# Second layer's attention: query projections moved to the second and third step of a batch

## The reference, cut to what matters

```python
x = x + _attention(_rmsnorm(x, g1), wq, wk, wv, wo)      # this stage
# in _attention, per batch:
q = (x @ wq).reshape(B, S, 16, 16).transpose(0, 2, 1, 3) # query projections
k = (x @ wk)...; v = (x @ wv)...                         # 4 heads each
q = q * cos + _rotate_half(q) * sin                      # rotary turn
k = k * cos + _rotate_half(k) * sin
scores = einsum('bhqd,bhkd->bhqk', q, k) / sqrt(16), causal
out = softmax(scores) @ v ... @ wo
```

## Time and profile before

| | |
|---|---|
| three timed runs | 3857.84, 3857.79, 3856.64 us; median 3857.79 |
| profiled execution | 3857.93 us, its span 3856.1 us |
| TensorE busy, share of the span | 3439.5 us, 89% |
| VectorE, ScalarE, GpSimd busy | 2474.5, 2175.3, 1169.2 us |
| mean granted TensorE clock | 0.938 of full speed |

### The profile page before, as it was taken

How to read it: one execution, slowest core, us unless ns; L and a number is a source line. 1 busy time by engine, 2 the same in 40 slices (tenths; PEclk the granted TensorE clock), 3 DMA queues, 4 the chain that set the end, 5 groups by cost and what they waited for, 6 DMA issues and landing times. The chain is left out here.

```text
span 3856.1 us, 68147 instructions
## 1 busy us (share of the span) xinstructions
PE 3439.5 (89%) x19130; PEld 2597.4 (67%) x19130; DVE 2474.5 (64%) x7055; ACT 2175.3 (56%) x5066; POOL 1169.2 (30%) x1802
## 2 busy tenths in 40 slices
PE   2999999999999999989999968867878775799996
PEld 2777777777777777768888834445555555688885
DVE  5777777777777777766666633345555545566665
ACT  1777777777777777746555521124545441355553
POOL 1333333333333333333343300032122200343442
PEclk9999999999999999999999967878989895899998
DMA  4222222222222222243343311110001014355454
GB/s 156 44 48 48 48 48 48 48 48 48 46 45 46 48 48 48 48 162 122 120 142 120 120 39 33 33 40 20 24 22 25 21 28 151 120 137 137 118 140 150
DMA packets 177636, 282.42 MB, mean 73 GB/s; under 512 B 32498, under 2 KB 119282, under 8 KB 177522
## 3 DMA queue, kind: packets, MB, share of 16 engines
q1 hardware_dynamic: 162930, 261.03, 23.4%
q0 software_dynamic: 14592, 19.93, 3.1%
HBM read 161.89 MB, written 41.16 MB: 53 GB/s over the span
## 5 line engine op out<-in xcount | busy, mean ns | idle before, releaser
L723 POOL TENSOR_SCALAR at_p<-at_p,at_recip 128x128 f32<-128x128 f32 (+3 forms) x1028 | 533.6, 532 | 983.3 <-DVE at_recip L862 983.3
L773 ACT ACTIVATE at_p<-at_p,at_nmax 128x128 f32<-128x128 f32 (+3 forms) x1030 | 575.8, 559 | 290.4 <-DVE at_nmax L856 287.3
L856 DVE CUSTOM_DVE_ANT_0 at_p<-at_s_ps,at_bias 128x128 f32<-128x128 f32 (+3 forms) x1030 | 493.7, 479 | 154.1 <-PE at_s_ps L971 154.1
L978 PE MATMUL at_t_ps<-ident,at_p 128*128 128x128 f32 x2560 | 459.7, 278 | 0.4 <-POOL at_p L723 0.4
L1745 DVE CUSTOM_DVE_ANT_0 aa_a_ps<-aa_a_ps,aa_hidden 128x128 f32<-128x128 f32 (+3 forms) x512 | 247.2, 507 | 273.7 <-PE aa_a_ps L1909 269.7
L970 PE MATMUL at_s_ps<-at_k_twice,at_q 128*128 128x128 f32 (+3 forms) x1030 | 387.8, 377 | 8.1 <-DVE at_nmax L856 1.2
L1645 ACT ACTIVATE aa_pT<-aa_b_ps 128x512 f32<-128x512 f32 (+1 forms) x384 | 196.2, 528 | 281.8 <-PE aa_b_ps L1927 277.8
L971 PE MATMUL at_s_ps<-at_k_twice,at_q 128*128 128x128 f32 (+3 forms) x1030 | 332.3, 323 | 0.0
L978 PEld LDWEIGHTS at_t_ps<-ident,at_p 128*128 128x128 f32 x2560 | 294.9, 140 | 46.2 <-DVE at_pT L869 30.0
L988 PE MATMUL at_o_ps<-at_pT,at_v 128*64 128x512 f32 (+3 forms) x2064 | 306.3, 439 | 0.0
L970 PEld LDWEIGHTS at_s_ps<-at_k_twice,at_q 128*128 128x128 f32 x1030 | 194.4, 189 | 91.0 <-DVE at_nmax L856 44.5
(11 more groups left out here) (316 smaller groups left out, 8639.1 us busy)
## 6 DMA issues: line engine op xcount, KB each, us to landing
at_k_twice<-at_k_parts SPq DMA_DIRECT2D x260, 256.0 KB, 3.3
nw_w_raw<-in_w_all_dram SPq DMA_DIRECT2D x52, 1024.0 KB, 7.5
w_raw<-in_w_dram SPq DMA_DIRECT2D x57, 768.0 KB
ln_x<-in_x_dram SPq DMA_DIRECT2D x10, 512.0 KB, 4.8
nw_xh<-xh_dram SPq DMA_DIRECT2D x10, 512.0 KB, 4.3
nw_xl<-xl_dram SPq DMA_DIRECT2D x10, 512.0 KB, 4.9
rc_x<-x_dram SPq DMA_DIRECT2D x10, 512.0 KB, 3.8
at_w_raw<-in_w_heads_dram SPq DMA_DIRECT2D x18, 256.0 KB, 3.4
```

What stands on the lines that cost most here:

```text
L723: pool.tensor_scalar(p, p, recip[:, u:u + 1], 1.0, ALU.mult, ALU.mult).then_inc(scaled, 1)
L773: act.activation(p_sb[:, u, 0:N], p_sb[:, u, 0:N], ACT.Exp, bias=nmax[:, u:u + 1], scale=-1.0, accum_out=total[:, u:u + 1]).then_inc(exped, 1)
L856: dve.tensor_tensor_reduce(out=p_sb[:, u, 0:N], in0=s_ps[u % 2][:, 0:N], in1=bias[:, u % 2, S - N:S], scale=1.0, scalar=BIG, op0=ALU.add, ...
L978: ins = pe.transpose(t_ps[u % 2][:, k * P:k * P + P], p_sb[:, u, k * P:k * P + P], ident[:])
```

## The change

The table NEXT is rewritten. q0 goes from (2,0) to (1,1), q1 from (10,0) to (2,1), kk from (1,1) to (2,0); p0 from (4,1) to (6,1), p1 from (5,1) to (7,1), p2 and p3 to (8,1) and (10,0), k1 from (6,0) to (9,1), k2 and k3 to (11,0) and (12,1), p4 from (12,1) to (12,0). x0, x1, v, k0, M0, p5, p6 and p7 stay, and the work in each job is the same. `low_k` follows its key projection from the end of step 2 to the end of step 3, and two of the four `make_xr` go from steps 11 and 12 to 9 and 10. Both exchanges of a batch now stand in the same turn of SyncE's loop, q0's ahead of `pack`, q1's behind it, and each has its own semaphore.

```diff
-        exchanged = sem("aa_exchanged")
+        exchanged = [sem(f"aa_exchanged{m}") for m in range(2)]
...
-        NEXT = {(0, 0): "x0", (0, 1): "x1", (1, 1): "kk", (2, 0): "q0", (4, 0): "k0", (3, 1): "v", (4, 1): "p0", (5, 1): "p1",
...
+        NEXT = {(0, 0): "x0", (0, 1): "x1", (1, 1): "q0", (2, 0): "kk", (2, 1): "q1", (3, 1): "v", (4, 0): "k0",
+                (6, 1): "p0", (7, 1): "p1", (8, 1): "p2", (9, 1): "k1", (10, 0): "p3", (11, 0): "k2", (12, 0): "p4",
...
-                    sp.dma_start(turn2[to:to + QUARTER, m, :], turn1[of:of + QUARTER, m, :]).then_inc(exchanged, 16)
+                    sp.dma_start(turn2[to:to + QUARTER, m, :], turn1[of:of + QUARTER, m, :]).then_inc(exchanged[m], 16)
...
             exchange(1, 0)
+            exchange(1, 1)
             for G in range(GROUPS):
                 if G + 2 < GROUPS:
                     place(G + 2)
                 n, g = divmod(G + 1, KV1)
-                if g % 2 == 0 and n + 1 < B:
-                    exchange(n + 1, g // 2)
+                if g == 0 and n + 1 < B:
+                    exchange(n + 1, 0)
                 pack(G)
+                if g == 0 and n + 1 < B:
+                    exchange(n + 1, 1)
                 spread_out(G)
...
-                pool.wait_ge(exchanged, 64 * (2 * n + m + 1))
+                pool.wait_ge(exchanged[m], 64 * (n + 1))
...
-                    if s == 2 and n + 1 < B:
+                    if s == 3 and n + 1 < B:
                         low_k(n + 1)
-                    if s in (11, 12, 14, 15) and n + 2 < B:
-                        make_xr(n + 2, (11, 12, 14, 15).index(s))
+                    if s in (9, 10, 14, 15) and n + 2 < B:
+                        make_xr(n + 2, (9, 10, 14, 15).index(s))
```

More of the change, by code:

```diff
@@ L1466, in attention_phase @@
         FIRST = ["x0", "x1", "kk", "q0", "k0", "p0", "p1", "v", "q1", "k1", "p2", "p3", "M0", "k2", "k3", "p4", "p5", "p6", "p7"]
-        NEXT = {(0, 0): "x0", (0, 1): "x1", (1, 1): "kk", (2, 0): "q0", (4, 0): "k0", (3, 1): "v", (4, 1): "p0", (5, 1): "p1",
-                (6, 0): "k1", (7, 1): "p2", (9, 1): "p3", (10, 0): "q1", (10, 1): "k2", (11, 0): "k3", (12, 1): "p4",
-                (13, 0): "M0", (13, 1): "p5", (14, 0): "p6", (15, 0): "p7"}
+        NEXT = {(0, 0): "x0", (0, 1): "x1", (1, 1): "q0", (2, 0): "kk", (2, 1): "q1", (3, 1): "v", (4, 0): "k0",
+                (6, 1): "p0", (7, 1): "p1", (8, 1): "p2", (9, 1): "k1", (10, 0): "p3", (11, 0): "k2", (12, 0): "p4",
+                (12, 1): "k3", (13, 0): "M0", (13, 1): "p5", (14, 0): "p6", (15, 0): "p7"}
         SAME = {(1, 0): "M1", (5, 0): "M2", (9, 0): "M3"}
```

## The result

The changed kernel takes 3755.07 us (median of four runs, 3753.36 to 3755.62) against 3857.82 us of the kernel before in the same job: ratio 0.9733, 95% interval 0.9716 to 0.9749. The spans of the two profiles differ by 102.2 us, the seven batches that prepare a next one by 104.5.

The account below looks back on a forecast made before the run. It took TensorE's waits for GpSimd's late-starting work at the query spreads, with no other engine near its limit, as the bound; -67.6 - 30.6 - 9.3 + 17 + 2 + 5 = -83.5 from 3857.93 gave 3774 us, range 3750 to 3810.

Parts of the forecast that it names:

- The stops at p0 and p4: TensorE's 14 waits for GpSimd at the query spreads in steps 4 and 12 both go: -67.6 us.
- The clock behind them: Half clock in the 5 us windows behind the 14 query-spread waits comes back to full: -30.6 us.
- Rival (e): Attention stage ends slower because denser work is granted a lower clock, 0.81: 3871 us; chance 0.03.
- `part` in step 12: TensorE's 1.55 us mask wait behind part, slowed beside GpSimd's product, goes in six batches: -9.3 us.
- ScalarE's peak: Two key copies in steps 10 and 11 taken apart: up to 0.5 us a batch, 3 us, left at nothing.
- What comes in step 4: low_k ahead of k0, low_k and part held by GpSimd: 2.4 us a batch, +17 us; clock there +5 us.
- rival (b): Waits move into step 4, held instructions at full price, clock falling in every batch: 3803 us; chance 0.14.
- `norm` in step 6: norm falls into GpSimd's turn of q1 and can be late by 0 to 1.3 us: +2 us (0 to 9).
- Rival (c): VectorE and ScalarE used the stops to catch up; half of 67.6 us returns as mask waits: 3808; chance 0.06.
- Rival (d): p0 in step 6 waits again as q0's way grows; only p4's waits go: 3822 us; chance 0.04.
- signs named for being right: No query-spread wait over 1 us, period 64 to 66, no half clock behind steps 4 and 12, k0 wait 1.4 to 2.7.
- (a): The forecast itself, 3755 to 3795 us by the ends of its terms taken singly; chance 0.72.

Follow-up runs that it names:

- the runs with one part each: Kernel before with only q1 projected early, 3785.98 us against 3859.38; kernel before with only p0 to p3 and k1 to k3 moved later, 3812.05 us against 3859.38.
- the run with p0 late only: Kernel before with p0 moved to step 6, p1, p2, p3 to steps 7, 9, 11, projections and exchanges unmoved: 3812.05 us against 3859.38.
- the last run: Changed kernel with kk back in step 1 ahead of q0 in step 2, low_k back at the end of step 2: 3742.7 us against 3857.65.
- the run with k0 in step 5: Changed kernel with k0 in slot 1 of step 5 instead of slot 0 of step 4, low_k unmoved: 3750.39 us against 3859.38.
- the run with GpSimd behind `low_k`: Changed kernel with one more wait, so GpSimd's turn of q0 begins when low_k of the same batch is done: 3758.3 us against 3857.65.
- `low_k` in step 4: Changed kernel with low_k at the end of step 4 and k0 in slot 0 of step 6: 3741.22 us against 3859.38.
- with xr early: Kernel with low_k at the end of step 4 and k0 in step 6, plus make_xr in steps 9, 10, 11, 13: 3740.74 us against 3857.65.

## Why the prediction was right, and what it mis-sized

- The stops at p0 and p4: forecast -67.6 us, and the trace shows no wait at the query spreads. The margin at step 6, forecast as 3.8 us, is 5.4 in batch 2: GpSimd ends at 2736.24 and p0's spread starts at 2741.68, with step 4 itself 1.2 us longer than reckoned. The waits at the two places are gone in the runs with one part each, too.
- The clock behind them: forecast -30.6 us, measured 33.0 us over 7 us windows of before. My 5 us windows cut off the ends of the eight longest. Rival (e), a lower clock for denser work, is out: 404 us of work in 432 us ran at 0.98.
- `part` in step 12: forecast -9.3. Step 12 falls to 3.6 us and its `part` takes 0.18 + 0.18.
- ScalarE's peak, left at nothing, gave 3.3 us: seven waits of 0.47 for an exponential in step 12 before, none after. That the two key copies make them is not shown: the run with p0 late only has both copies where they were, with p3 between them and the step, and none of these waits.
- What comes in step 4, the step that failed in size: forecast +17 us for the delay and +5 for the clock. The wait at k0 is 1.82 us (2.14 in batch 0), inside the 1.4 to 2.7 that were named. But the further delay that I added, of the third score part behind the held `part`, is nothing: `part` was held for 0.3 us, not 1.9, and its score part, behind the delayed k0, no longer waited. An undisturbed step 4 takes 5.0 us where the run with p0 late only takes 3.7: 1.3 us a batch, less in batch 0, and not 2.4, so 8 us for 17. I had taken the value near the row of step 12, where GpSimd's long products had just begun; here its short instructions lay beside it. The clock cost 8.2 us for 5. That is half of rival (b), the falling clock, in four batches of seven and not in all; the full hold of each instruction did not come.
- `norm` in step 6: forecast +2, and step 6 grew by 1.8 us (23.6 for 21.8), but not for this reason, so the match is luck. `norm` was held in batches 1, 5 and 6 (1.06 to 1.08 us) and not in 2 to 4 (0.69), and batch 0 has none there, yet step 6 takes 3.37 or 3.38 us in all seven, and step 7 3.96 in 1 to 6. The hold cost nothing here; what lengthened step 6 stays open.
- Missed: step 3 loses 6.5 us, 4.8 of them since `low_k` no longer stands ahead of its first mask (by the last run); where the other 1.7 come from is open. The change moved an instruction on VectorE, and I priced only the place to which it went. Rows 8 had shown it, at 2754.52 at the head of step 3.
- Rival (c), half of the idle time coming back as mask waits, is refuted: these fell from 25.8 to 9.5 us. Rival (d) did not occur.
- Of the signs named for being right, two failed: the period is 61.2 to 64.1 us and not 64 to 66, and windows at half clock stand behind step 4, 0.50 in batch 5.
- The upper end of (a), 3795, does not follow from the terms of the sum: taken singly they reach 3786, all together 3803.

By terms over the seven batches: the profiles' 104.5 us are 67.6 (stops), 16.3 (masks, of which step 12 is 9.2) and 3.3 (ScalarE) of TensorE's idle time, less 13.1 at k0, and 33.0 - 8.2 = 24.8 of clock: 98.9. The remaining 5.6 us are not in the waits: TensorE's busy time in the batches fell by 31.2 us, 6.4 more than the clock explains, and I leave these open. The 21 us between this and the sum of 83.5 are step 4 (9), step 3 (6.5), ScalarE (3.3), and 2 of small items.

## What to carry to other kernels

In a list of jobs written out by hand, the distance between a job and its use has to be compared with the whole way between them, here 15.4 us for a projection whose use stood two and a half steps of 4 us on; the price of such a stop was here its idle time and, on TensorE, half as much again for the clock behind it (33.0 for 67.6 us). When an instruction is moved on an in-order engine, price the place that it leaves as well as the one to which it comes. A wait named at one instruction may only be the first look at a longer chain: moving k0 alone gave 2 us in the batches' sum of the profiles (431.3 to 429.5), moving what fed it as well gave 13 (417.9).

## What the runs showed of the hardware

- The granted clock fell to its lower level behind TensorE's waits of 1.8 to 2.1 us in four of seven batches of the changed kernel, behind 1.7 to 2.0 us in three of the run with k0 in step 5, and behind 1.54 us in five of the run with GpSimd behind `low_k`, with the same instructions in all batches. In the three runs whose longest wait in these batches was 0.99 us (`low_k` in step 4, with xr early or not) or 1.36 us (kk first) it fell in none. What tells the batches apart is not shown by any run.
- VectorE instructions with two SBUF inputs and the small tensor_scalar took longer beside a GpSimd instruction: the second of `part` 1.25 us for 0.18, ending with it, `low_k` 0.97 to 1.29 for 0.69, `norm` up to 1.82 for 0.69. GpSimd's were held by VectorE's (0.94 for 0.61, 1.60 for 1.28). A reciprocal and the masks beside the same instructions kept their 0.25 and 0.3 to 0.7 us. This agrees with the exclusive lock of the Trainium skill (SBUF — State Buffer, Who interferes with whom), also for `low_k` and `norm`, for which no row before had shown it.
